# Sort phase of a graph layer: the lane one-hot of a lot in two operations and the products of slots and pieces in four

## The reference

```python
edge_index = jnp.stack([src, dst])
...
row, col = (edge_index[0], edge_index[1])
...
deg = jax.ops.segment_sum(ew_sl, row_sl, num_segments=N)
...
msgs = xw[col_sl] * norm[:, None]
h7 = jax.ops.segment_sum(msgs, row_sl, num_segments=N) + b
```

## Time and profile before

| | us |
|---|---|
| median of 3 runs | 4299.95 (4298.56 to 4305.78) |
| the profiled execution | 4323.12 |
| its span, first to last instruction | 4321.4 |
| sort: first lane one-hot to the last scatter's end | 97.6 to 732.5 |
| mean granted TensorE clock | 0.842 |

### The profile page before, as it was taken

The page is one execution under the profiler, slowest core; times in us unless marked ns, Lnnn a source line. Parts: engine busy times, 40 slices in busy tenths (PEclk is TensorE's granted clock), DMA queues, the critical chain, the costliest instruction groups (busy, mean ns, idle before and its releaser), DMA issues. The chain is left out here.

```text
span 4321.4 us, 76641 instructions
## 1 busy us (share of the span) xinstructions
PE 3243.9 (75%) x20540; PEld 2558.6 (59%) x20541; DVE 2762.1 (64%) x7406; ACT 1568.4 (36%) x4966; POOL 2673.6 (62%) x2429
## 2 busy tenths in 40 slices
PE   5788775756777677767557777777778579999995
PEld 4566554724444444444436566665656469999985
DVE  7999997845555555556545555555555665555577
ACT  1777773511111111111003333333333255555552
POOL 1888886256666666666666666666666236666663
PEclk8888887578888888888778888888888789999998
DMA  4322222543333333333334444444444412222367
GB/s 157 47 28 27 26 28 46 166 130 109 110 110 109 108 111 109 110 108 111 100 92 128 128 127 131 129 129 130 127 128 130 156 40 70 70 70 70 119 215 274
DMA packets 292325, 466.66 MB, mean 108 GB/s; under 512 B 96007, under 2 KB 197900, under 8 KB 292239
## 3 DMA queue, kind: packets, MB, share of 16 engines
q0 software_dynamic: 139776, 272.98, 24.2%
q1 hardware_dynamic: 143727, 187.23, 13.0%
q10 hardware_dynamic: 8738, 5.43, 0.4%
HBM read 361.91 MB, written 104.56 MB: 108 GB/s over the span
## 5 line engine op out<-in xcount | busy, mean ns | idle before, releaser
L1711 POOL DMA_INDIRECT rows<-table,idx x1664 | 1590.6, 956 | 912.2 <-issue 495.0
L2013 DVE TENSOR_TENSOR acc<-acc,ps_seg 128x256 f32 x1664 | 696.6, 419 | 951.4 <-remote 791.6
L2178 PE MATMUL ps_seg<-rows,pick 128*128 128x256 f32 x3328 | 1004.4, 431 | 375.0 <-DVE acc L2013 289.2
L2178 PEld LDWEIGHTS ps_seg<-rows,pick 128*128 128x128 f32 x3328 | 666.5, 214 | 554.5 <-issue 464.3
L885 POOL DMA_INDIRECT records<-sort_rec,sort_addr x280 | 531.6, 1899 | 185.1 <-DVE sort_rec L1020 94.1
L1855 DVE TENSOR_SCALAR pick<-iota_row,loc,ewt 128x128 f32<-128x128 f32 x1680 | 526.9, 363 | 13.7 <-remote 9.2
L2631 POOL DMA_INDIRECT y_rows<-arena,spot x204 | 295.9, 1451 | 207.0 <-issue 61.8
L2773 PE MATMUL ps_h<-arena,up_now 128*128 128x128 f32 x3264 | 401.1, 277 | 4.0 <-DVE up_now L2701 2.0
L2773 PEld LDWEIGHTS ps_h<-arena,up_now 128*128 128x128 f32 x3264 | 382.2, 193 | 7.4 <-issue 7.3
L2757 PE MATMUL ps_y<-down_now,arena 128*128 128x256 f32 x1632 | 385.9, 380 | 0.0
L1083 PE MATMUL ps_out<-acc 128*128 128x240 bf16 x1568 | 265.7, 350 | 122.0 <-DVE acc L1004 121.9
(11 more groups left out here) (408 smaller groups left out, 4920.1 us busy)
## 6 DMA issues: line engine op xcount, KB each, us to landing
rows<-table,idx POOLq DMA_INDIRECT x1664
acc<-y_rows SPq DMA_DIRECT2D x20, 896.0 KB
x_early<-in_x SPq DMA_DIRECT2D x118, 128.0 KB
xn<-in_x SPq DMA_DIRECT2D x100, 128.0 KB
xT_dram<-xT SPq DMA_DIRECT2D x98, 128.0 KB
xn<-xT_dram SPq DMA_DIRECT2D x49, 256.0 KB
skip<-in_x SPq DMA_DIRECT2D x98, 128.0 KB
x_rows<-acc SPq DMA_DIRECT2D x49, 256.0 KB
```

The source lines that it names most:

```text
L1711: pool.indirect_dma_start(out=rows[:, t, :], out_offset=None, in_=k.table, in_offset=bass.IndirectOffsetOnAxis(idx[:, h, t:t + 1], 0)).the ...
L2013: dve.tensor_tensor(here, here, sums(u), ALU.add).then_inc(added[u], 1)
L2178: last = pe.matmul(sums(t), pick[:, h, t, :], rows[:, t, :], start=True, stop=True)
```

## The change

The lane one-hot is made by two instructions, one per side of 14 columns, and the products by four: for each side three of the six pieces at a time. The elements written, their values and their order within the buffers stay. `lane_done` now rises by two a lot and `valued_done` by four (`VALUED`, with the credit raised to 8), and PE waits at the first column of each side for that side's lanes and for both of its products.

```diff
--- before.py
+++ after.py
@@ -837,7 +837,10 @@
             "act_ranked").split())
         BY_DVE = RANK_BANKS - BANKS_BY_ACT
         COLS_BY_ACT = RANK_COLS * BANKS_BY_ACT
-        REDUCED_CREDIT, PICK_CREDIT, ONE, TWO, VALUED_CREDIT = BY_DVE, COLS_BY_ACT, 1, 2, 2 * SIDES
+        REDUCED_CREDIT, PICK_CREDIT, ONE, TWO = BY_DVE, COLS_BY_ACT, 1, 2
+        FEW_PIECES = PIECES // 2
+        VALUED = SIDES * (PIECES // FEW_PIECES)
+        VALUED_CREDIT = 2 * VALUED
         SCATTERS = 16 * GROUPS_OUT
         cols = lambda g: range(g * RANK_COLS, min((g + 1) * RANK_COLS, LOT))
         pairs = lambda a: a.rearrange("p (n two) -> p n two", two=2)
@@ -930,7 +933,7 @@
 
                 def body(n, h, i, left, with_x=False):
 
-                    act.wait_ge(valued_done, SIDES * (n - 1) + VALUED_CREDIT)
+                    act.wait_ge(valued_done, VALUED * (n - 1) + VALUED_CREDIT)
                     for side in range(SIDES):
                         act.activation(piece2[:, h, side, :, :, :],
                                        s.pieces[:, :, bass.ds(n * LOT + side * SIDE, SIDE)].unsqueeze(3).to_broadcast(
@@ -989,10 +992,12 @@
 
                 def routes(n, h):
                     dve.wait_ge(lane2_done, n + 1)
-                    dve.tensor_tensor(in_lane[:, h, :, :].rearrange("p c (l two) -> p c l two", two=2),
-                                      pairs(s.iota_b).unsqueeze(1).to_broadcast([P, LOT, P // 2, 2]),
-                                      lane2[:, :, :].unsqueeze(2).to_broadcast([P, LOT, P // 2, 2]),
-                                      ALU.is_equal).then_inc(lane_done, 1)
+                    for side in range(SIDES):
+                        c = slice(side * SIDE, (side + 1) * SIDE)
+                        dve.tensor_tensor(in_lane[:, h, c, :].rearrange("p c (l two) -> p c l two", two=2),
+                                          pairs(s.iota_b).unsqueeze(1).to_broadcast([P, SIDE, P // 2, 2]),
+                                          lane2[:, c, :].unsqueeze(2).to_broadcast([P, SIDE, P // 2, 2]),
+                                          ALU.is_equal).then_inc(lane_done, 1)
                     dve.wait_ge(slot2_done, n + 1)
                     dve.tensor_tensor(in_slot[:, :, :].rearrange("p c (s two) -> p c s two", two=2),
                                       pairs(s.iota_b[:, 0:SLOTS_OUT]).unsqueeze(1).to_broadcast([P, LOT, SLOTS_OUT // 2, 2]),
@@ -1001,12 +1006,14 @@
                     dve.wait_ge(eq_done, n + 1)
                     for side in range(SIDES):
                         dve.wait_ge(piece2_done, SIDES * n + side + 1)
-                        dve.tensor_tensor(
-                            valued[:, h, side, :, :, :].rearrange("p v c (s two) -> p v c s two", two=2),
-                            in_slot[:, side * SIDE:(side + 1) * SIDE, :].rearrange("p c (s two) -> p c s two", two=2).unsqueeze(
-                                1).to_broadcast([P, PIECES, SIDE, SLOTS_OUT // 2, 2]),
-                            piece2[:, h, side, :, :, :].unsqueeze(3).to_broadcast([P, PIECES, SIDE, SLOTS_OUT // 2, 2]),
-                            ALU.mult).then_inc(valued_done, 1)
+                        for few in range(0, PIECES, FEW_PIECES):
+                            v = slice(few, few + FEW_PIECES)
+                            dve.tensor_tensor(
+                                valued[:, h, side, v, :, :].rearrange("p v c (s two) -> p v c s two", two=2),
+                                in_slot[:, side * SIDE:(side + 1) * SIDE, :].rearrange("p c (s two) -> p c s two", two=2).unsqueeze(
+                                    1).to_broadcast([P, FEW_PIECES, SIDE, SLOTS_OUT // 2, 2]),
+                                piece2[:, h, side, v, :, :].unsqueeze(3).to_broadcast([P, FEW_PIECES, SIDE, SLOTS_OUT // 2, 2]),
+                                ALU.mult).then_inc(valued_done, 1)
 
                 def lift(n):
                     dve.wait_ge(moved_done, n + 1 + TWO)
@@ -1074,12 +1081,12 @@
                     last.then_inc(moved_done, 1)
 
                 def compact(n, h):
-                    pe.wait_ge(lane_done, n + 1)
                     pe.wait_ge(rec_done, n + ONE)
                     for c in range(LOT):
                         side, at = c // SIDE, c % SIDE
                         if at == 0:
-                            pe.wait_ge(valued_done, SIDES * n + side + 1 + VALUED_CREDIT)
+                            pe.wait_ge(lane_done, SIDES * n + side + 1)
+                            pe.wait_ge(valued_done, VALUED * n + VALUED // SIDES * (side + 1) + VALUED_CREDIT)
                         last = pe.matmul(OUT, in_lane[:, h, c, :], valued[:, h, side, :, at, :], start=(c == 0),
                                          stop=(c == LOT - 1))
                     last.then_inc(out_done, 1)
```

## The result

| | before | with the change |
|---|---|---|
| median | 4299.47 us (4295.72 to 4305.78, 16 runs) | 4306.56 us (4302.06 to 4315.09, 16 runs) |
| ratio | | 1.0019, 95% interval 1.0011 to 1.0026 |
| profiled execution, span | 4321.4 us | 4304.1 us |
| first lane one-hot to the last scatter's end | 97.6 to 732.5, 634.9 us | 97.1 to 743.1, 646.0 us |

The change costs 7.1 us, 0.19%, where 9.1 was forecast. It is slower, and its interval (4.7 to 11.2 us) holds the forecast. The 16 runs and the trace do not say the same: the sort itself grew by 11.2 us in the trace. The two spans can't be compared as wholes, since the gathering stage differs by 27 us between these two executions (2540 and 2513 us), and that stage is not touched.

The account below looks back on a forecast made before the run. The prediction took DVE, busy 97 of every 100 us, to bound the sort. Added instructions +11.3 us and POOL's end -2.2 us sum to +9.1 us on 4300.0, so 4309 us, range 4302 to 4318.

Parts of the forecast that it names:

- DVE sets the pace of a lot: In the sort, DVE never waits for another engine; three added instructions cost 0.07 us each over 54 lots, +11.3 us.
- PE's earlier start: PE asks for one side's lanes only, but its last awaited product comes 0.14 us later; gain nothing, 1.37 us cover stays.
- POOL's end: After the `rec` of lot 53, POOL's waits in the last lots fall from 4.2 to 1.9 us: -2.2 us.
- A start at +0.9: A scatter starting 0.9 us into the lane one-hot falls just behind its middle and still waits about 1.0 us.
- one near 2.5: Sign in POOL's trace: the scatters of 2.6 and 2.4 us replaced by one near 2.5, others under 2.3.
- Register work on PE and ACT: PE computes one more awaited value per side while waiting anyway, ACT's awaited products are long done; cost nothing.
- Rival B: More collisions: a scatter's read delays small DVE operations by 0.05 us, up to 10.8 us on top, 4320 us; chance 0.12.
- Rival A: POOL also holds DVE, and shorter pieces win back its idle 0.3 us a lot, 16 us: 4293 us; chance 0.10.
- C: POOL's waits at the sort's end only move and give nothing back: 4311 us; chance 0.12.
- D: PE starts earlier, which shortens a lot and covers DVE's added time: 4300 us; chance 0.04.
- no change can be told from a change under 0.2%: For the whole kernel's time, differences under 0.2%, 8.6 us, count as no change; the forecast lies just above.

Follow-up runs that it names:

- thirteen more: Lane one-hot in four and products in twelve, 13 DVE instructions a lot more than the kernel before; +51.3 us, ratio 1.0135.
- one small operation less: Kernel before with the low bits of a position masked and joined with the high ones in one DVE operation instead of two; -1.4 us, ratio 0.9996.
- the repeat: The change measured once more against the kernel before, in the follow-up runs; +7.5 us, ratio 1.0017.
- the padded loop: Kernel before with two semaphore increments a lot more on DVE, which nobody waits for; +7.0 us, ratio 1.0016.

## Why the prediction was right or wrong

- *DVE sets the pace of a lot, and an added instruction lies fully on the path at 0.07 us.* Right: 0.069 for the lane and 0.071 for each product in the change, 0.069 and 0.069 with thirteen more. 54 x 0.211 = 11.4 for 11.3.
- *PE's earlier start is worth nothing, its cover stays.* Right: in the change no DVE row waits for PE before the last two lots.
- *POOL's end gives back 2.2.* 1.6 in the first trace (30.9 after the `rec` of lot 53 for 32.5), 0.5 in the second. Right in kind, too large in size: a part of the holds moved to the last lots' products (2.41, 2.35 and 2.36).
- *A start at +0.9 falls behind the middle of the lane one-hot and still waits 1.0.* Wrong, and so was the sign "one near 2.5": a first scatter that starts 0.95 after the lane one-hot comes just before the second piece and is not held, and in the lots behind a turn, where it starts at +0.73, it is held for 0.23. Between lots 2 and 52 no scatter took more than 2.22, and POOL's holds fell from 1.8 us a lot to 0.3. It cost the forecast nothing, since nobody waits for POOL there.
- *Register work on PE and ACT costs nothing.* Nothing in the traces speaks against it. But the turn of DVE's own loop got dearer, by 0.14 us in 26 turns, +3.6, and the sum had no term for it.
- *Not in the sum either*: L983 no longer meets a scatter, 54 x -0.04 = -2.2. Rival B had seen this collision, and took its sign wrong: the change has fewer.
- The sort comes to 11.4 - 2.2 + 3.6 - 1.6 = +11.2, measured +11.2. The forecast of 9.1 lies 2.1 under that and 2.0 over the total of +7.1. That it was near the sort is in part luck, since two missing terms, +3.6 and -2.2, nearly cancelled; that it was near the total is luck as well, as far as the 4 us by which the total stays under the sort are unexplained.
- *Rival A, the hold is mutual.* True as a mechanism: the casts show it, up to 0.3 us a time. But in the kernel before one lot in 56 has a held cast (the means are 0.189 and 0.195), so there was nothing to win, and DVE's idle 3% are waits for its own results, as the run with one small operation less shows. *C* (the end gives nothing back) is not refuted: 1.6 and 0.5 lie between it and the forecast. *D* is refuted by the list of waits.
- That no change can be told from a change under 0.2% was too strict: the interval of this 0.19% leaves zero out with 16 runs of each kernel, and ten or eleven were enough for the repeat and for the padded loop.

## What to carry to other kernels

Where an engine is busy for 97% of a stage, count its instructions: each further one costs its fixed part (0.07 us here), and a small operation whose result the very next one needs costs 0.12 us more; put other work between the two before looking for operations to leave out. Long DVE operations on two SBUF operands hold POOL's indirect DMAs, and these can hold a DVE cast, so before lengthening, shortening or reordering one, add up POOL's lot with its holds: at 11.05 of 11.17 us nothing was lost, a product of twice the length cost 113 us, and a quicker DVE gained 3 us (5 in the sort) of the 13 that its own time promised. Compare one trace on the stage that the change touches, since other stages vary by more than a small change is worth.

## What the runs showed of the hardware

- The hold, in both directions. A scatter that starts inside a long two-operand DVE operation ends 1.51 us after the next operation starts (held for 2.5 us by the product of 3.58). A cast that starts 0.53 to 0.79 us after a scatter waits up to 0.3 us and ends 1.04 to 1.08 us after the scatter's start; one that starts in its first 0.5 us is not held. The Trainium skill, SBUF — State Buffer, section Who interferes with whom, says that a DVE instruction with two SBUF inputs contends with GpSimd's reads, and that `cast` can take the shared pair; the traces agree with both, with one difference: only a part of POOL's instruction is in a cast's way, not the whole 1.55 us. With short pieces a scatter can wait for more than one. With thirteen more, the one below starts inside the eleventh product, which gives way 0.35 us later, and is held to the end of the twelfth, at 408.00, and 1.51 more:

```profile
407.29 2.22 POOL L889 DMA_INDIRECT records<-sort_rec,sort_addr  x1 [0.30 <-issue]
```

- The turn of DVE's loop takes 0.17 to 0.20 us or 0.32 from the branch to the first register operation, by where the loop lies in the instruction stream, with the same body length (62) on either side.
- The kernel before takes 3916 and 3920 us on two chips and 4332 on a third, and 4299 in the first measurement. The sort is equal to 0.3 us in the two profiles of it. The difference is in gathering: from 1500 to 2500 us the granted TensorE clock is 0.82 in the first profile and 0.92 in the second chip's, as means over times at 1.2 and times at 2.4 GHz. Here are these stretches, first of the kernel before as profiled first, then of its repeat on the second chip:

```profile
1500.00:2500.00 1000.00, 691.53 (x2512) 482.78 (x2511) 565.27 (x1807) 185.25 (x389) 642.38 (x671) 0.82 0.38 111
```

```profile
1500.00:2500.00 1000.00, 845.63 (x3217) 547.15 (x3218) 672.28 (x2145) 270.25 (x513) 759.23 (x790) 0.92 0.47 137
```

In the same 1000 us the second chip issues 3217 matmuls where the first has 2512. Whether the clock is the cause or both follow from something else was not tried.
